# Decoder layer: two heads per output strip and the bias on GpSimd in self-attention; maxima transposed inside the by-key block and fills spread out in cross-attention

## The chip, the cores and the metric

The kernel runs on one core of a Trainium2 chip. The time is device microseconds of one execution. The engines are TensorE (PE; its weight loads are shown as PEld), VectorE (DVE), ScalarE (ACT), GpSimd (POOL) and SyncE (SP), which issues the DMAs. Each has its own instruction stream, and they wait for one another on semaphores.

## The reference

64 sequences of 128 tokens with 128 features, and for each a context of 77 tokens, pass through one decoder layer in float32:

```
x = x + self_attention(layernorm(x))                 # causal, 16 heads of 8, rotary q and k
x = x + cross_attention(layernorm(x), ctx, ctx)
x = x + experts(layernorm(x))                        # top 2 of 8 low-rank experts

self:  out = softmax(q @ k.T * 8**-0.5 + causal) @ v @ Wo + bo
cross: scores = q @ k.T / sqrt(8);  probs = softmax(scores)
       feats = [mean(scores), mean(max_k scores), mean(var_k probs)]   # per sequence and head
       t = exp(clip(mlp(feats), log 0.1, log 10))
       out = softmax(q @ k.T / (2 t)) @ v @ Wo + bo
```

## The kernel before

There are three parts with a barrier between them, and the residual stream X stays on chip: self-attention (about 34 to 547 us), cross-attention (551 to 1285 us) and the experts. The change touches the first two. In both, each engine runs a loop of steps over the 64 sequences, written out by hand: step n does one stage for sequence n, another for n+1, a third for n-3 and so on, and the order of the calls in `step` is the order of the instructions on that engine. A semaphore wait stands at the start of each call. An engine takes its instructions strictly in order.

**Self-attention, step n on PE** (`both_scores`, `pv`, `on_transpose`, `project`, ...). Scores are computed twice, in chunks of 8 heads (h = 0, 1): by query (SQ, to find each row's maximum, with the causal mask added by a matmul, line 436) and by key (SK, from which ACT takes the exponential into P, line 283). Each uses the two PSUM banks of its own tile, so the next chunk's matmuls wait until DVE's maximum (line 356) or ACT's exponential has read the last. P times V goes to O: 16 matmuls of 32 output rows per sequence, where head 4g + j has the strip of rows 32j and the column block g, so O has four blocks of 128 columns. ACT copies O (128x512) to `o`, PE transposes the four blocks (line 485) into R, DVE divides by the sums, PE transposes the result, and `project` adds two products into L: a row of ones times the bias (line 496, contraction over one row) and the output weights (line 497). DVE then adds L to X (line 373) and takes the statistics for the next layer norm. Within a step the order after the first half's P times V is: transpose of xn(n+3), transpose of on(n-2), project(n-3), qkv(n+3), transpose of the maxima(n+1). qkv's stationary operand is xnT, which ACT copies out of PSUM (line 268) after the exponential of chunk 0. POOL makes masked copies of keys and queries, three multiplications a step.

**Cross-attention.** Its parts are split by a lag. For sequence n (`scores_outer`, `scores_inner`) the scores by query go to SQ; DVE takes the row maxima (lines 936, 938) into FEAT; PE transposes them (line 1096) into O; ACT copies them negated into mT (line 809); PE subtracts them from the scores (line 1101); ACT takes the exponential, POOL squares it, DVE sums both. For each group of 8 sequences a small MLP (`mlp1`, `mlp2`, `mlp3`) gives the temperatures. Eleven steps later (LAG) the same sequence is done by key: `by_key(b, h)` is two products of `shift` with `pick` (contraction over 128 rows, line 1112) and three pairs of products over 32 rows (line 1116); then the exponential (line 836), P times V, transpose, norm, projection (lines 1154, 1155). So in steps 0 to 10 only the first half of the work is there, in steps 11 to 63 both, and after that only the second. The maxima of n are transposed before `by_key(n - LAG, 1)`.

ACT's order in a cross step is: exponential of chunk 0, scaled query and row, copies of xcT and o, the maxima (mT), the copies of q, k and v (`qkv_copy`), exponential of chunk 1, copy of onT (line 846), the exponential of the scores.

Before its first step, cross-attention fills its tiles: POOL sets VA (128x7950) and P (128x4096); DVE sets HK, LK, mT and shift, and prepares the MLP's weights; ACT makes `pick`, `heads` and a rounded bias. PE, POOL and DVE each wait for the fills of the others before the first step; DVE's first layer norm (line 920) stands behind all of its own.

Of the kernel before, what the change touches and what calls it, by code (L numbers as in the profile page):

```python
# [15 lines left out]
QUADS, JH = 4, 4  # L16
# [6 lines left out]
def need(eng, sem, value):  # L23
# [10 lines left out]
    headmask=([128, JH], F32, "headmask"), wo=([C, C], F32, "L0_attn_Wo"), bo=([1, C], F32, "L0_attn_bo"),  # L34
# [18 lines left out]
def load_constants(sp, tiles, loaded, constants, dram):  # L53
    for name, (shape, _, source) in constants.items():
# [5 lines left out]
        if name == "b3":  # L60
            src = src.to_broadcast(shape)
# [68 lines left out]
def self_attention(nc, X, ST, MEAN, RSTD, constants, loaded):  # L130

    RING = 4
    ctx = ExitStack()
    with ctx:
# [6 lines left out]
        def sem(name):  # L141
# [4 lines left out]
        ident, identb, identm, future, causal, headmask, cos, sin, wqkv, wo, bo = (  # L146
            constants[n] for n in ("ident", "identb", "identm", "future", "causal", "headmask", "cos", "sin", "wqkv",
                                   "wo", "bo"))
        ones_row = sb("ones_row", [1, T])
# [8 lines left out]
        VA = sb("VA", [128, RING, H, 32])  # L158
# [8 lines left out]
        o = sb("o", [128, QUADS * T])  # L167
# [6 lines left out]
        xn_ready = sem("xn_ready")  # L174
        xnT_ps = sem("xnT_ps")
# [42 lines left out]
        SETS = 3  # L218
        SPLIT = 6
# [17 lines left out]
        def _(pool):  # L237
            nc.gpsimd.memset(VA[:], 0.0).then_inc(const_set, 1)
            pool.wait_ge(const_set, 1)
            nc.gpsimd.memset(VA[:, :, :, DK:DK + 1], 1.0).then_inc(const_set, 1)  # L240
            nc.gpsimd.memset(ones_row[:], 1.0).then_inc(const_set, 1)
# [14 lines left out]

            def step(n, k, i):
                if real(n + 2):
                    masks(n + 2, (k + 2) % RING)

# [3 lines left out]
        def _(act):  # L264
# [5 lines left out]
            def v_copy(b, k):  # L270
                act.wait_ge(rope_part, 3 * (b + 1))
                need(act, pv_ps, 2 * b - 6)
                nc.scalar.copy(VA[:, k, :, 0:DK], M[:, 2 * C:3 * C].rearrange("k (h d) -> k h d", d=DK)).then_inc(v_sb, 1)

# [53 lines left out]
        def _(dve):  # L328
# [30 lines left out]
            def norm(b):  # L359

                dve.wait_ge(oT_ps, b + 1)
                sums = R[:].rearrange("q (h e) -> q h e", e=32)
                nc.vector.reciprocal(rinv[:], sums[:, :, DK]).then_inc(o_rinv, 1)
                dve.wait_ge(o_rinv, b + 1)
                need(dve, onT_ps, b)
                nc.vector.tensor_tensor(on[:].rearrange("q (h d) -> q h d", d=DK), sums[:, :, 0:DK],
                                        rinv[:].unsqueeze(2).to_broadcast([128, H, DK]),
                                        ALU.mult).then_inc(o_norm, 1)
# [33 lines left out]
        def _(pe):  # L402
# [65 lines left out]
            def pv(b, h, k):  # L468
# [4 lines left out]
                for a in range(2):  # L473
                    g = 2 * h + a
                    for j in range(JH):
                        last = mm(O[32 * j:32 * j + 32, g * T:(g + 1) * T], VA[:, k, JH * g + j, :],
                                  P[:, 2 * (k % 2) + h, (JH * a + j) * T:(JH * a + j + 1) * T],
                                  start=(g == 0), stop=(g == QUADS - 1), skip_group_check=True)
# [13 lines left out]
            def project(b):  # L492
# [3 lines left out]
                mm(L[:, T:T + C], ones_row[:], bo[:], start=True, stop=False)  # L496
                mm(L[:, T:T + C], onT[:], wo[:], start=False, stop=True).then_inc(proj_ps, 1)
# [29 lines left out]
def cross_attention(nc, X, ST, MEAN, RSTD, constants, loaded, dram):  # L527

    GROUP = 8
    SLOTS = 2 * GROUP  # L530
    ROUNDS = B // GROUP
    LAG = 11
# [4 lines left out]
    R8 = float(DK) ** 0.5  # L537
    ctx = ExitStack()
    with ctx:
# [66 lines left out]
        const_set = sem("const_set")  # L606
        act_set = sem("act_set")
        pads = sem("pads")
# [54 lines left out]
        SETS = 5  # L663
        PADS = 4
# [15 lines left out]
        def of_group(tile, r):  # L680
            p = r % 2
# [8 lines left out]
        def _(sp):  # L690
# [6 lines left out]
            def rows(b):  # L697
                sp.wait_ge(row_sb, b + 1)
# [7 lines left out]
            sp.wait_ge(pads, PADS)  # L706
# [1164 lines left out]
```

## Time and profile before

| | us |
|---|---|
| median of 3 runs | 1848.47 (1848.45 to 1857.84) |
| profiled execution, its own time | 1853.18 |
| its span | 1851.4 |
| PE busy in the span | 1695.9 |
| DVE busy | 1238.7 |
| ACT busy | 921.6 |
| POOL busy | 848.8 |

The profile is one execution. Busy time is an engine's own; PE's weight loads overlap its matmuls. A matmul's shown time is from its start to the end of its results, so that matmuls that follow one another closely overlap. The clock is TensorE's granted one as a share of 2.4 GHz: 1.00 is 2.4 and 0.50 is 1.2 GHz. Over the whole span its mean is 0.913. In brackets behind a row stands how long the engine was idle just before it and what ended that; `issue` is a time in which the profile shows nothing that it waited for.

### The profile page before, as it was taken

How to read it: one execution, taken by the hardware profiler on the slowest of the kernel's cores; microseconds unless marked ns; L12 is line 12 of the kernel's file. 1: busy time of each engine (PE TensorE's matmuls, PEld its weight loads, DVE VectorE, ACT ScalarE, POOL GpSimd, SP SyncE). 2: the span in 40 equal slices, each digit the busy share in tenths (PEclk: the TensorE clock that was granted, in tenths of full speed). 3: DMA queues.
4: the chain of work that ended last, by engine and by line, in shares of the span. 5: the costliest groups of instructions: out<-in, count | busy, mean ns of one | idle time of the engine just before them, and what ended most of it. 6: DMA issues, size and time to landing. Idle time of an engine off the chain costs nothing. (4 is left out here: it accounts for less than half of the span.)

```text
span 1851.4 us, 42638 instructions
## 1 busy us (share of the span) xinstructions
PE 1695.9 (92%) x14420; PEld 1267.3 (68%) x14420; DVE 1238.7 (67%) x2792; ACT 921.6 (50%) x2143; POOL 848.8 (46%) x892
## 2 busy tenths in 40 slices
PE   0999999999976799999999999886899999999998
PEld 0455555555544566666666666543899999999998
DVE  4666666666655656777777777312777787778776
ACT  1455555555542345666666665433554545454543
POOL 0433444443325556777667776320343344334432
PEclk9999999999985558999999999655899999999999
DMA  5000000000000000000000000000000000000000
GB/s 161 2 2 1 1 1 1 1 1 1 1 6 6 5 4 6 7 7 7 7 6 8 6 7 4 2 2 1 4 7 9 9 9 6 9 9 9 6 9 13
DMA packets 26311, 16.50 MB, mean 9 GB/s; under 512 B 6179, under 2 KB 23525, under 8 KB 26213
## 3 DMA queue, kind: packets, MB, share of 16 engines
q1 hardware_dynamic: 26212, 15.23, 2.9%
q8 instruction: 58, 0.95, 0.2%
q14 instruction: 41, 0.33, 0.1%
HBM read 9.97 MB, written 4.19 MB: 8 GB/s over the span
## 5 line engine op out<-in xcount | busy, mean ns | idle before, releaser
L836 ACT ACTIVATE xa_P<-xa_SK 77x1024 f32<-77x1024 f32 x128 | 130.6, 1020 | 161.8 <-PE xa_SK L1116 161.8
L283 ACT ACTIVATE sa_P<-sa_SK 128x1024 f32<-128x1024 f32 x128 | 131.2, 1025 | 147.2 <-PE sa_SK L426 147.2
L249 POOL TENSOR_TENSOR sa_KM<-sa_HQK,sc_headmask 128x512 fp32r<-128x512 f32 x64 | 66.5, 1039 | 292.1 <-ACT sa_HQK L278 292.1
L1394 POOL TENSOR_TENSOR ff_zz<-ff_zt 128x256 f32<-128x256 f32 x32 | 38.4, 1199 | 319.8 <-DVE ff_zt L1591 319.8
L1462 ACT ACTIVATE ff_SG<-bank 128x512 f32<-128x512 f32 x128 | 76.8, 600 | 192.0 <-PE bank L1664 191.8
L1581 DVE TENSOR_TENSOR ff_GL<-ff_GU,ff_GH 128x512 fp32r<-128x512 f32 x128 | 147.4, 1171 | 27.5 <-ACT ff_GH L1467 27.2
L356 DVE TENSOR_REDUCE sa_mx<-sa_SQ 128x8 f32<-128x1024 f32 x128 | 156.5, 1223 | 6.8 <-PE sa_SQ L426 5.4
L770 POOL TENSOR_TENSOR xa_QMH<-xa_QBH,xc_headmask 128x512 fp32r<-128x512 f32 x64 | 72.7, 1136 | 190.8 <-ACT xa_QBH L826 190.8
L1729 PE MATMUL bank<-fh_r,ff_GH 128*128 128x256 f32 x512 | 148.4, 290 | 0.0
L1662 PE MATMUL bank<-ff_ZH,fh_b 128*128 128x256 f32 x512 | 147.7, 289 | 0.0
L1663 PE MATMUL bank<-ff_ZL,fh_b 128*128 128x256 f32 x512 | 145.1, 283 | 0.0
L1664 PE MATMUL bank<-ff_ZH,fl_b 128*128 128x256 f32 x512 | 144.9, 283 | 0.0
L1731 PE MATMUL bank<-fh_r,ff_GL 128*128 128x256 f32 x512 | 143.6, 280 | 0.0
L728 POOL TENSOR_TENSOR xa_E<-xa_E 128x1232 f32<-128x1232 f32 x64 | 143.1, 2236 | 0.2 <-ACT xa_E L818 0.2
L1730 PE MATMUL bank<-fl_r,ff_GH 128*128 128x256 f32 x512 | 143.0, 279 | 0.0
L1576 DVE TENSOR_TENSOR ff_GU<-ff_SG,bank 128x512 f32<-128x512 f32 x128 | 88.0, 688 | 68.6 <-ACT ff_SG L1462 63.1
L1467 ACT CAST ff_GH<-ff_GU 128x512 fp32r<-128x512 f32 x128 | 79.0, 624 | 55.3 <-DVE ff_GU L1576 32.1
L936 DVE TENSOR_REDUCE xa_FEAT<-xa_SQ 128x12 f32<-128x924 f32 x64 | 71.7, 1121 | 51.8 <-PE xa_SQ L1071 51.6
L1112 PE MATMUL xa_SK<-xa_shift,xa_pick 128*128 128x512 f32 x256 | 104.8, 495 | 0.0
L1402 POOL TENSOR_TENSOR ff_ZH<-ff_AH,ff_M 128x512 fp32r<-128x512 f32 x64 | 83.3, 1302 | 45.9 <-ACT ff_M L1440 45.9
L445 PE MATMUL sa_SK<-sa_shift,sa_pick_row 128*128 128x512 f32 x256 | 103.8, 486 | 0.0
L1663 PEld LDWEIGHTS bank<-ff_ZL,fh_b 128*128 128x128 f32 x512 | 98.4, 192 | 0.0
(257 smaller groups left out, 5444.1 us busy)
## 6 DMA issues: line engine op xcount, KB each, us to landing
xa_shift<-xa_row SPq DMA_DIRECT2D x256, 2.0 KB
out<-X SPq DMA_DIRECT2D x64, 64.0 KB, 1.5
xa_cx<-ctx SPq DMA_DIRECT2D x64, 38.5 KB
sa_shift<-sa_mT SPq DMA_DIRECT2D x64, 8.0 KB, 1.8
fr_b<-L_ffn_B SPq DMA_DIRECT2D x2, 256.0 KB, 3.9
fr_r<-down_a SPq DMA_DIRECT2D x1, 512.0 KB, 4.7
fr_w<-L_ffn_w_gate SPq DMA_DIRECT2D x1, 256.0 KB, 3.5
fr_w<-L_ffn_w_up SPq DMA_DIRECT2D x1, 256.0 KB, 3.6
```

The lines of the kernel that those rows point to most:

```text
L283: nc.scalar.activation(P[:, 2 * (k % 2) + h, :], SK[:], ACT.Exp).then_inc(p_ready, 1)
L356: nc.vector.tensor_reduce(mx[:, p, 2 * JH * h:2 * JH * h + 2 * JH], SQ[:].rearrange("q (j k) -> q j k", k=T), AX.X, ALU.max).then_inc(max_ ...
L728: nc.gpsimd.tensor_tensor(E2[:], E1[:, b % 2], E1[:, b % 2], ALU.mult).then_inc(e2_ready, 1)
L836: nc.scalar.activation(P[0:TC, (2 * b + h) % 4, :], SK[0:TC, :], ACT.Exp).then_inc(p_ready, 1)
L1112: mm(bank(SK, a), pick[:, r // 32], shift[:, b % 2].rearrange("c j t -> c (j t)"), start=True, stop=False)
L1581: nc.vector.tensor_tensor(GG[1][:, k % 4, :], GU[:, k % 2, :], GG[0][:, k % 4, :].bitcast(F32), ALU.subtract).then_inc(gl_done, 1)
L1662: mm(out, w[0], x[0], start=start, stop=False, **kw)
L1663: mm(out, w[0], x[1], start=False, stop=False, **kw)
L1664: return mm(out, w[1], x[0], start=False, stop=stop, **kw)
L1729: mm(out, h, RD[0][:, f, :], start=(s == 0 and f == 0), stop=False, skip_group_check=True)
L1730: mm(out, h, RD[1][:, f, :], start=False, stop=False, skip_group_check=True)
L1731: last = mm(out, l, RD[0][:, f, :], start=False, stop=(s == 1 and f == 3), skip_group_check=True)
```

## The change

In self-attention two heads share a strip of O. V is laid out in two halves per sequence, one for the even heads and one for the odd, with zeros where the other head's columns are, so that the products of both heads add up in the same 32 rows. O then has two blocks of 128 columns, and `o_copy`, `o_transpose` and `norm` follow. The bias is added to X by POOL (`add_bias`), one sequence a step, after xn has been taken; the bias matmul goes, and the residual on DVE waits for POOL as well.

In cross-attention `by_key(b, 1)` takes a function that it calls after its first pair of 32-row products; it holds the transpose of the maxima and the MLP's third product. The fills are spread: POOL sets the V tile of the first four sequences and mT before its first step, the rest of V at step 0, and a quarter of P in each of the steps 1 to 4; DVE prepares the MLP's weights at step 0, splits the bias at step 2 and sets the padding columns of HK and LK and the tile shift at steps 2 to 4; ACT makes `heads` at step -2 and `pick` at step 1. Each has a semaphore of its own, and waits for it where it is first used. Some constants get names (RINGS, HIDDEN) with their values unchanged; the group stays at 8.

```
# self-attention
-        VA = sb("VA", [128, RING, H, 32])
+        VA = sb("VA", [128, RING, 2, PART])            # PART = 265
-        o = sb("o", [128, QUADS * T])
+        o = sb("o", [128, 2 * T])
+            def add_bias(b):                            # POOL
+                pool.wait_ge(xn_ready, b + 1)
+                xb = X[:, bass.ts(b, C)]
+                nc.gpsimd.tensor_tensor(xb, xb, bo_rows[:], ALU.add).then_inc(biased, 1)
             def step(n, k, i):
                 if real(n + 2):
                     masks(n + 2, (k + 2) % RING)
+                if real(n + 1):
+                    add_bias(n + 1)
-                nc.scalar.copy(o[:], O[:]).then_inc(o_sb, 1)
+                nc.scalar.copy(o[:], O[:, 0:2 * T]).then_inc(o_sb, 1)
             def residual(b):
                 dve.wait_ge(proj_ps, b + 1)
+                dve.wait_ge(biased, b + 1)
-                for a in range(2):
-                    g = 2 * h + a
-                    for j in range(JH):
-                        last = mm(O[32 * j:32 * j + 32, g * T:(g + 1) * T], VA[:, k, JH * g + j, :],
...
+                for e in range(2):
+                    for t in range(4):
+                        head = 2 * t + e
+                        at = 256 * e + 32 * (4 * h + t)
+                        last = mm(O[32 * t:32 * t + 32, h * T:h * T + T], VA[:, k].rearrange("k e x -> k (e x)")[:, at:at + 32],
...
-                for g in range(QUADS):
-                    last = tr(R[:, g * T:(g + 1) * T], o[:, g * T:(g + 1) * T], ident[:])
+                for h in range(2):
+                    last = tr(R[:, h * T:(h + 1) * T], o[:, h * T:(h + 1) * T], ident[:])
-                mm(L[:, T:T + C], ones_row[:], bo[:], start=True, stop=False)
-                mm(L[:, T:T + C], onT[:], wo[:], start=False, stop=True).then_inc(proj_ps, 1)
+                mm(L[:, T:T + C], onT[:], wo[:], start=True, stop=True).then_inc(proj_ps, 1)
# cross-attention, by key and the step on PE
+                    if part == 0 and between is not None:
+                        between()
...
-                if real(n):
-                    max_transpose(n)
-                if r is not None:
-                    mlp3(r)
+                def maxima():
+                    if real(n):
+                        max_transpose(n)
+                    if r is not None:
+                        mlp3(r)
                 if real(n - LAG):
-                    by_key(n - LAG, 1)
+                    by_key(n - LAG, 1, maxima)
+                else:
+                    maxima()
# cross-attention, fills
+            values(0, FIRST, 0)                         # POOL, before its steps; FIRST = 4
+            nc.gpsimd.memset(mT[:].bitcast(F32), 0.0).then_inc(mT_set, 1)
...
+                if n == 0:
+                    values(FIRST, VRING, 2)
+                if 1 <= n <= 4:
+                    nc.gpsimd.memset(P[:, n - 1], 0.0).then_inc(p_set, 1)
+                if n == 0:                              # DVE, at the end of its step
+                    prepare()
+                if n == 2:
+                    split_bias()
+                    nc.vector.memset(HK[:, :, TC:T].bitcast(F32), 0.0).then_inc(pads_set, 1)
+                if n == 3:
+                    nc.vector.memset(LK[:, :, TC:T].bitcast(F32), 0.0).then_inc(pads_set, 1)
+                if n == 4:
+                    nc.vector.memset(shift[:].bitcast(F32), 0.0).then_inc(shift_set, 1)
```

PE's order in self-attention, from the second half's P times V to qkv, before and now (line numbers of each kernel's own text; the two middle parts are the other half's scores):

```order
L476 MATMUL sa_O<-sa_P,sa_VA 32x128 x7
L485 MATMUL sa_R<-sc_ident,sa_o 128x128 [waits sa_onT_sb,sa_o_sb]
L485 MATMUL sa_R<-sc_ident,sa_o 128x128 x3
L421 MATMUL sa_M<-sc_ident,sa_qk 128x128 [waits sa_v_sb,sa_qk_roped]
...
L490 MATMUL sa_R<-sc_ident,sa_on 128x128 [waits sa_o_norm]
L496 MATMUL sa_L<-sc_bo,sa_ones_row 128x128 [waits sa_mT_sb,sa_x_done,sa_onT_sb]
L497 MATMUL sa_L<-sc_wo,sa_onT 128x128
L416 MATMUL sa_M<-sc_wqkv,sa_xnT 128x384 [waits sa_xnT_sb]
```

```order
L489 MATMUL sa_O<-sa_P,sa_VA 32x128 x7
L498 MATMUL sa_R<-sc_ident,sa_o 128x128 [waits sa_onT_sb,sa_o_sb]
L498 MATMUL sa_R<-sc_ident,sa_o 128x128
L433 MATMUL sa_M<-sc_ident,sa_qk 128x128 [waits sa_v_sb,sa_qk_roped]
...
L503 MATMUL sa_R<-sc_ident,sa_on 128x128 [waits sa_o_norm]
L509 MATMUL sa_L<-sc_wo,sa_onT 128x128 [waits sa_mT_sb,sa_x_done,sa_onT_sb]
L428 MATMUL sa_M<-sc_wqkv,sa_xnT 128x384 [waits sa_xnT_sb]
```

Two of the four transposes of o and the bias product are gone; their waits stand on what follows.

PE's order in a cross step, from the transposes of o to the subtraction of the maxima, before and now:

```order
L1144 MATMUL xa_R<-xc_ident,xa_o 128x128
L1096 MATMUL xa_O<-xc_ident,xa_FEAT 16x128 [waits xa_o_sb,xa_max_ready]
L1112 MATMUL xa_SK<-xa_shift,xa_pick 128x512 [waits xa_p_ready]
L1112 MATMUL xa_SK<-xa_shift,xa_pick 128x512
L1116 MATMUL xa_SK<-xa_QMH,xa_HK 128x512 x2
L1116 MATMUL xa_SK<-xa_QML,xa_HK 128x512 x2
L1116 MATMUL xa_SK<-xa_QMH,xa_LK 128x512 x2
L1101 MATMUL xa_SQ<-xa_heads,xa_mT 128x462 [waits xa_mT_sb]
```

```order
L1188 MATMUL xa_R<-xc_ident,xa_o 128x128
L1153 MATMUL xa_SK<-xa_shift,xa_pick 128x512 [waits xa_p_ready]
L1153 MATMUL xa_SK<-xa_shift,xa_pick 128x512
L1157 MATMUL xa_SK<-xa_QMH,xa_HK 128x512 x2
L1131 MATMUL xa_O<-xc_ident,xa_FEAT 16x128 [waits xa_o_sb,xa_max_ready]
L1157 MATMUL xa_SK<-xa_QML,xa_HK 128x512 x2
L1157 MATMUL xa_SK<-xa_QMH,xa_LK 128x512 x2
L1138 MATMUL xa_SQ<-xa_heads,xa_mT 128x462 [waits xa_mT_sb]
```

The wait for `xa_max_ready` now stands behind four products instead of ahead of them, and between the maxima's transpose and the subtraction there are four products instead of eight.

POOL's order at the start of cross-attention now:

```order
L735 MEMSET xa_VA 128x2120
L738 MEMSET xa_VA 77x8x8 [waits xa_va_set]
L743 MEMSET xa_mT 128x2048
L775 TENSOR_TENSOR xa_LK<-xa_QK,xa_HK 128x77 [waits xa_h_ready,xc_loaded]
...
L784 TENSOR_TENSOR xa_KML<-xa_LK,xc_headmask 128x308 [waits xa_l_ready]
L735 MEMSET xa_VA 128x5830
L738 MEMSET xa_VA 77x22x8 [waits xa_va_set]
L750 TENSOR_TENSOR xa_E<-xa_E 128x1232 [waits xa_e1_ready]
```

Before, one memset of 7950 columns and one of P stood ahead of the first `xa_LK`; now the larger part of V is set between the masks of step 0 and the first square.

## Rows read from the trace of the kernel before

**Rows 1.** By stretch: us, busy us of PE, PEld, DVE, ACT, POOL, clock, DMA, GB/s
```profile
300.00:400.00 100.00, 100.00 (x948) 59.09 (x943) 69.24 (x158) 50.72 (x105) 40.71 (x41) 1.00 0.01 1
...
660.00:700.00 40.00, 39.43 (x207) 27.45 (x206) 20.52 (x35) 15.64 (x43) 23.32 (x27) 0.50 0.02 6
...
704.00:708.00 4.00, 4.00 (x52) 2.76 (x42) 1.63 (x2) 1.86 (x3) 0.00 (x0) 0.77 0.01 4
...
800.00:900.00 100.00, 93.45 (x873) 63.67 (x873) 73.70 (x146) 65.11 (x171) 72.11 (x88) 0.98 0.03 7
...
1200.00:1240.00 40.00, 36.26 (x217) 20.09 (x217) 5.57 (x20) 12.08 (x24) 8.55 (x8) 0.50 0.01 2
```

**Rows 2.** Timeline, one self step, PE: start us, us, engine, line, op, [idle]
```profile
297.90 0.66 PE L485 MATMUL sa_R<-sc_ident,sa_o 128*128 128x128 f32 x4
...
301.06 0.33 PE L412 MATMUL sa_M<-sc_ident,sa_xn 128*128 128x128 f32 x1
...
301.43 0.48 PE L496 MATMUL sa_L<-sc_bo,sa_ones_row 1*128 1x128 f32 x2
...
301.84 0.49 PE L497 MATMUL sa_L<-sc_wo,sa_onT 128*128 128x128 f32 x2
...
302.06 0.30 PEld L416 LDWEIGHTS sa_M<-sc_wqkv,sa_xnT 128*128 128x128 f32 x2
...
305.52 0.66 PE L485 MATMUL sa_R<-sc_ident,sa_o 128*128 128x128 f32 x4
```

**Rows 3.** Timeline, the same self step: what PE waits for next
```profile
296.99 1.22 DVE L356 TENSOR_REDUCE sa_mx<-sa_SQ 128x8 f32<-128x1024 f32 x1
...
298.50 0.21 PEld L436 LDWEIGHTS sa_SQ<-sc_causal,sc_identb 128*128 128x128 bf16 x2
...
301.60 0.26 ACT L268 COPY sa_xnT<-sa_M 128x128 f32<-128x128 f32 x1
```

**Rows 4.** Timeline, starts of both attention parts, POOL and DVE
```profile
34.15 1.80 POOL L238 MEMSET sa_VA<- 128x2048 f32 x1 [33.70 <-POOLq L74]
...
34.20 1.84 DVE L332 TENSOR_SCALAR sa_xn<-X,MEAN,RSTD 128x128 f32<-128x128 f32 x1 [9.29 <-PEq L74]
...
551.42 6.71 POOL L717 MEMSET xa_VA<- 128x7950 f32 x1
...
563.28 0.33 DVE L920 TENSOR_SCALAR xa_xn<-X,MEAN,RSTD 128x128 f32<-128x128 f32 x1
```

**Rows 5.** Timeline, one cross step, PE
```profile
849.98 0.52 PEld L1101 LDWEIGHTS xa_SQ<-xa_heads,xa_mT 128*128 128x128 f32 x3 [0.36 <-issue]
...
856.33 0.38 PE L1144 MATMUL xa_R<-xc_ident,xa_o 128*128 128x128 f32 x2
...
857.27 0.28 PE L1096 MATMUL xa_O<-xc_ident,xa_FEAT 128*16 128x128 f32 x1 [0.56 <-DVE xa_FEAT L938]
...
857.30 0.71 PE L1112 MATMUL xa_SK<-xa_shift,xa_pick 128*128 128x512 f32 x2
...
857.94 0.50 PE L1116 MATMUL xa_SK<-xa_QMH,xa_HK 32*128 32x512 f32 x2
...
858.84 0.52 PEld L1101 LDWEIGHTS xa_SQ<-xa_heads,xa_mT 128*128 128x128 f32 x3 [0.37 <-issue]
...
860.28 0.32 PE L1154 MATMUL xa_M<-xa_bias,xa_minus_ones 2*128 2x128 f32 x1
```

**Rows 6.** Timeline, the same cross step, ACT
```profile
857.59 0.27 ACT L809 ACTIVATE xa_mT<-xa_O 16x128 fp32r<-16x128 f32 x1 [1.95 <-PE xa_O L1096]
...
858.95 1.02 ACT L836 ACTIVATE xa_P<-xa_SK 77x1024 f32<-77x1024 f32 x1 [0.30 <-PE xa_SK L1116]
...
859.87 0.25 ACT L846 COPY xa_onT<-xa_R 128x128 f32<-128x128 f32 x1
```

**Rows 7.** Timeline, ACT: maxima copies of two neighbouring cross steps
```profile
685.26 0.27 ACT L809 ACTIVATE xa_mT<-xa_O 16x128 fp32r<-16x128 f32 x1 [3.02 <-PE xa_O L1096]
...
699.74 0.27 ACT L809 ACTIVATE xa_mT<-xa_O 16x128 fp32r<-16x128 f32 x1 [3.02 <-PE xa_O L1096]
```

More of the change, by code:

```diff
@@ L730, in similarity @@
             def similarity(r):
-                part = slice(r % 2 * GROUP, r % 2 * GROUP + GROUP)
+                part = slice(r % RINGS * GROUP, r % RINGS * GROUP + GROUP)
                 pool.wait_ge(k_sb, GROUP * (r + 1))
-                need(pool, mlp_ps, 3 * (r - 2) + 1)
+                need(pool, mlp_ps, 3 * (r - RINGS) + 1)
                 nc.gpsimd.tensor_tensor(qk[:], qsum[:, part], ksum[:, part], ALU.mult).then_inc(qk_ready, 1)
@@ L742, in variance @@
                 cols = slice(slot(2 * i) * H, slot(2 * i) * H + 2 * H)
-                need(pool, mlp_ps, 3 * (2 * i // GROUP - 2) + 1)
+                need(pool, mlp_ps, 3 * (2 * i // GROUP - RINGS) + 1)
                 pool.wait_ge(zr_ready, i + 1)
@@ L750, in low @@
             def low(b):
-                need(pool, pads, PADS)
                 pool.wait_ge(h_ready, 2 * b + 2)
@@ L801, in qkv_copy @@
                                      accum_out=ksum[:, s:s + 1]).then_inc(k_sb, 1)
+                if b < VRING:
+                    act.wait_ge(va_set, 2 if b < FIRST else 4)
                 need(act, pv_ps, 2 * (b - VRING) + 2)
@@ L833, in exps @@
                 need(act, pv_ps, 2 * b + h - 3)
-                if b == 0 and h == 0:
-                    act.wait_ge(const_set, SETS)
+                if b < 2:
+                    act.wait_ge(p_set, 4)
                 nc.scalar.activation(P[0:TC, (2 * b + h) % 4, :], SK[0:TC, :], ACT.Exp).then_inc(p_ready, 1)
@@ L849, in gelu1 @@
                 act.wait_ge(mlp_ps, 3 * r + 1)
-                nc.scalar.activation(h1[:], R[0:64, 3 * T:4 * T], ACT.Gelu, bias=b1s[:]).then_inc(mlp_act, 1)
+                nc.scalar.activation(h1[:], R[0:64, HIDDEN], ACT.Gelu, bias=b1s[:]).then_inc(mlp_act, 1)
             def gelu2(r):
                 act.wait_ge(mlp_ps, 3 * r + 2)
-                nc.scalar.activation(h2[:], R[0:64, 3 * T:4 * T], ACT.Gelu, bias=b2[:]).then_inc(mlp_act, 1)
+                nc.scalar.activation(h2[:], R[0:64, HIDDEN], ACT.Gelu, bias=b2[:]).then_inc(mlp_act, 1)
             def inverse_t(r):
@@ L897, in _ @@
                     exp_e(n)
+                if n == -2:
+                    nc.scalar.copy(heads[:].rearrange("h (g k) -> h g k", k=TC),
+                                   ident[:, 0:H].unsqueeze(2).to_broadcast([128, H, TC])).then_inc(heads_set, 1)
+                if n == 1:
+                    nc.scalar.copy(pick[:], rows4.to_broadcast([128, QUADS, T])).then_inc(pick_set, 1)
+                    act.wait_ge(bias_ps, 1)
+                    nc.scalar.copy(bias_high[:], R[0:2, 0:C]).then_inc(bias_sb, 1)
         @block.vector
@@ L932, in row_max @@
                 dve.wait_ge(sq_ps, b + 1)
-                need(dve, mlp_ps, 3 * (b // GROUP - 2) + 1)
+                need(dve, mlp_ps, 3 * (b // GROUP - RINGS) + 1)
                 m = FEAT[:, 1, columns(b)]
@@ L963, in factors @@
             def factors(r):
-                part = slice(r % 2 * GROUP, r % 2 * GROUP + GROUP)
+                part = slice(r % RINGS * GROUP, r % RINGS * GROUP + GROUP)
                 dve.wait_ge(mlp_act, 3 * r + 3)
-                need(dve, row_sb, GROUP * (r - 1))
+                need(dve, row_sb, GROUP * (r - RINGS + 1))
                 nc.vector.tensor_scalar(CF[:], CF[:], math.exp(-LOG_T_MAX), None, ALU.max).then_inc(clipped, 1)
@@ L1103, in subtract_max, with by_key @@
                 last.then_inc(neg_ps, 1)
-            def by_key(b, h):
+            def by_key(b, h, between=None):
                 need(pe, p_ready, 2 * b + h)
+                if b == 0 and h == 0:
+                    pe.wait_ge(pads_set, 2)
+                    pe.wait_ge(shift_set, 1)
+                    pe.wait_ge(pick_set, 1)
                 if h == 0:
@@ L1161, in mlp1 @@
                 need(pe, onT_sb, n - LAG - 1)
+                if r == 0:
+                    pe.wait_ge(prepared, PREPARED + 1)
                 for f in range(3):
-                    last = mm(R[0:64, 3 * T:4 * T], w1s[:, f, :], of_group(FEAT[:, f], r), start=(f == 0), stop=(f == 2))
+                    last = mm(R[0:64, HIDDEN], w1s[:, f, :], of_group(FEAT[:, f], r), start=(f == 0), stop=(f == 2))
                 last.then_inc(mlp_ps, 1)
```

134 lines of the change are left out of this document (69 added, 65 removed).

## The prediction

> **What bounds the kernel now.** I read first the table by stretch, because the share over the whole span mixes stages that have different limits. In self-attention PE is busy all of the time and the other engines are not near it: DVE 69 us of 100, ACT 51, POOL 41 [rows 1]. So whatever PE issues there is paid for, until the next wait comes up. In the main part of cross-attention PE is busy 93 us of 100, and the rest is one wait, which repeats in each step. Between the two lies a stretch at 0.50 of the clock (1.2 GHz): the fills, the first steps of cross-attention, and about three of its full steps; the clock is back inside the stretch that starts at 704 us. The end of cross-attention (1200 to 1240 us) is at 0.50 again.
>
> Next I read the timeline of one step of each part, to see what stands behind PE. A self step takes 305.52 - 297.90 = 7.62 us [rows 2]. A cross step at 2.4 GHz takes 858.84 - 849.98 = 8.86 us, and PE idles 0.56 us in it, ahead of the transpose of the row maxima [rows 5].
>
> All sums are made against the profiled execution: 1853.18 us, with a span of 1851.4. The median of the runs is 1848.47, 4.7 us below it; I carry the difference over to the median unchanged.
>
> **Self: transposes of o, four to two.** Four take 0.66 us and one alone takes 0.33 [rows 2], so each one more costs (0.66 - 0.33) / 3 = 0.11, and two fewer save 0.22 us a step. Is PE held by something else 0.22 us earlier? The next instruction with a wait is the causal matmul: its weights load at 298.50, and the row maxima that free its bank end at 296.99 + 1.22 = 298.21 [rows 3]. A hand-over takes about 0.04 (the maxima transpose ends at 857.27 + 0.28 = 857.55 and ACT starts at 857.59 [rows 5, 6]). So the load moves to 298.28, and 298.25 would be its limit: the whole 0.22 is kept, but no slack is left. The product P times V keeps its count and its shape (two heads add into one strip, where each had its own), so it costs nothing. ACT's copy of o is halved, but that comes behind the copies for which PE waits.
>
> **Self: the bias matmul leaves PE.** From its first pass at 301.43 to the projection at 301.84 are 0.41 us [rows 2]. Behind it stand the projection and then the weights load of qkv, at 302.06, and this needs xnT, which ACT has ready at 301.60 + 0.26 = 301.86 [rows 3]. With 0.04 for the hand-over, qkv can't load before 301.90: only 302.06 - 301.90 = 0.16 of the 0.41 is gained, the rest becomes a wait for ACT, which is not free because it does an exponential ahead of that copy. (ACT's chain hangs on PE's score product, so it moves along with the 0.22 above.) The bounds are 0 and 0.41. I take 0.16, since the copy's end is a row and nothing in the change moves it. The addition goes to POOL, which is 59% idle there; the trace has no such operation in self, but even one as long as its 1.80 us memset [rows 4] fits, and the sequence's sum is wanted three steps later. The added wait in the residual stands ahead of the statistics on DVE and is met long before.
>
> Self together: (0.22 + 0.16) x 62 steps (of 64, the first and the last not being full ones) = 23.6 us. Bounds: 0.22 x 62 = 13.6, if the bias gives nothing, and 0.63 x 62 = 39.1.
>
> **Cross: the fills.** Now the first normalised x is ready at 563.28 + 0.33 = 563.61 [rows 4]; DVE's memsets and the weight preparation come before it. In the changed kernel it is DVE's first instruction. It won't start at once: in self-attention the same operation, started beside POOL's memset of 1.80 us, took 1.84 us instead of 0.33 and ended 0.09 after it [rows 4]. The Trainium skill (GPSIMD Engine Reference, Specifications) says that GpSimd's SBUF interfaces are shared with VectorE, with contention in its 2-port modes; the trace agrees by that 1.84. POOL's first VA memset now has 2120 columns, at 6.71 us / 7950 = 0.844 ns each, so it ends at 551.42 + 1.79 = 553.21, and x is ready at 553.3. Gain: 10.3 us. The price: POOL's second VA memset (5830 columns, 4.9 us) lies in step 0, behind the masks, and pushes the square, DVE's casts and its sum behind it by 1 us or so. Even with the full steps of 660 to 700 us DVE is idle 19.5 of 40 us and POOL 16.7 [rows 1], so most of it is made good in the next step. The P memsets are 1024 x 0.844 ns = 0.9 us each in POOL's idle time. I take off 0.5 and keep 9.8. Bounds: 7 (the memset's delay reaches PE in two steps) and 10.3.
>
> **Cross: maxima inside the second by-key block.** Now PE stops until 857.27 for the maxima. In the changed order the two mask products with shift, which need 857.94 - 857.30 = 0.64 to the next load [rows 5], start right behind the transposes of o, at 856.33 + 2 x 0.11 = 856.55, and the first product pair loads at 857.19 minus the little that the overlapping of the transpose took: 857.1. It lasts 0.50 [rows 5]. Then comes the price. At each change of the tile's rows PE's load waits for the pair in front to end: the load at 857.94 starts 0.07 before 857.30 + 0.71 = 858.01. The change adds two such points, before and behind the maxima transpose. So: transpose at 857.1 + 0.50 - 0.07 = 857.53, end 857.81 (the maxima are there at 857.23, no wait); next pair loads at 857.74, ends 0.50 later at 858.24; the last pair 0.23 later at 858.47; subtraction loads at 858.40, where it was 858.84. PE alone would gain 0.44.
>
> The Trainium skill (TensorEngine Tiling, Key Properties) says that changing the tiling mode, not just the tile, drains TensorE. The trace agrees by the 0.37 us idle ahead of the load at 858.84 [rows 5]. By the rule alone the two new drains of 0.37 would take back 0.74, more than the 0.56 that goes.
>
> But ACT is next. Its copy of the maxima moves from 857.59 to 857.85, by 0.26; behind it come the q, k and v copies and the exponential at 858.95, before which ACT idles 0.30 [rows 6]. So the exponential starts at 858.95 - 0.30 + 0.26 = 858.91, and the copy of onT, which ended at 859.87 + 0.25 = 860.12, ends at 860.08. The bias product that needs it starts at 860.12 in place of 860.28 [rows 5]: 0.16 a step. The bounds are -0.1 (the new drains cost 0.1 more than I read and ACT passes all on) and 0.44. I take 0.16, times 48 steps at 2.4 GHz: 7.7 us (bounds -5 and 21). In the three full steps at 1.2 GHz there is no wait to remove (39.43 of 40 us busy [rows 1]) and the two drains are pure loss, about 0.5 each: 1.5 us. The tail has no maxima: nothing.
>
> **Sum:** 23.6 + 9.8 + 7.7 - 1.5 = 39.6 us. Profiled about 1813.6, median 1848.5 - 39.6 = 1808.9 us.
>
> **The rivals.** (B) PE gets all that it is freed of: ACT's copies aren't last because its earlier work moves up too. 39.1 + 9.8 + 21 - 1.5 = 68 us, 1780. For it: ACT is only half busy; against it: the two hand-overs of [rows 3, 6]. (C) The time turns into waits: only the transposes count in self (13.6), the drains eat the gain in cross (-5), the fills give 7, less 1.5: 14 us, 1834. For it: there is no slack at 298.25, and the causal matmul may now wait; the shared port makes POOL's new addition and fills hold DVE. (D) slower: the clock comes back later. A cross step takes 699.74 - 685.26 = 14.48 us at 1.2 GHz [rows 7] against 8.86: 5.6 us for each step that the clock is late. PE was busy 39.43 of the 40 us before 700 and still at half clock [rows 1], so the return hangs on little, and the by-key block, dense before, now has two drains in it. From 7 steps late on the 40 us are gone; with 10 late it is 1848.5 - 40 + 56 = 1865 us. Against it: what PE executes in a step hardly differs. (E) the clock comes back up to three steps earlier: 17 us more, 1792. (F) The change doesn't do what it says, and another wait takes the place of that for the maxima without any gain: this is inside C.
>
> **How the numbers follow.** Forecast 0.60 (its own range 1797 to 1821), B 0.12, C 0.15, D 0.05, E 0.08. The range 1784 to 1832 leaves out about half of B, half of C, and D: under 0.2. A measurement of this kernel can tell about 0.5%, or 9 us, from no change. Faster by more than that: the forecast, B, E and most of C, 0.91; within it, a bad C or a D of five to eight steps, 0.04; slower, 0.05.
>
> **What would show it.** Self: a step of 7.24 us, two transposes of o, no bias product, and a new PE wait of about 0.25 us at qkv for ACT's xnT. Cross start: the first normalised x ready at 10.3 us less behind the start of its part than now, held by POOL's memset. Cross: a step of 8.70 us, no wait for the maxima, idle time of PE's loads on both sides of the maxima transpose, ACT without idle ahead of the second exponential, and PE waiting for the copy of onT. Wrong would be: a self step under 7.1 or over 7.4 us; a cross step under 8.5 or not under 8.86; or a stretch at half clock whose end does not move with the start of cross-attention.

## The result: 1794.05 us, about 58 us faster

The changed kernel took 1794.05 us (median of 4 runs, 1785.59 to 1797.58) beside 1852.47 for the kernel before in the same runs: ratio 0.968, interval 0.963 to 0.973. The forecast was 1808.9, with 1784 to 1832 as its range: right in sign, and the range held the time, but the gain was forecast at 39.6 us, and the time lies under the 1797 to 1821 that the prediction gave its main case. A second set of four runs of the same kernel gave 1802.16 (1793.78 to 1810.57), so the eight times together have a median of 1797 and a spread of 25 us. How much of a gain is the change and how much is such a spread is the main question of the experiments.

The profiled execution of after took 1791.54 us (span 1789.7), 61.6 less than the one of before. By stretch, in the columns of [rows 1]:

```profile
300.00:400.00 100.00, 96.68 (x925) 56.23 (x935) 74.20 (x168) 50.04 (x112) 48.05 (x57) 1.00 0.01 1
660.00:680.00 20.00, 19.80 (x181) 13.16 (x180) 15.09 (x30) 11.27 (x34) 16.71 (x21) 1.00 0.03 7
...
720.00:820.00 100.00, 97.68 (x924) 65.68 (x925) 74.58 (x148) 63.44 (x173) 76.06 (x95) 1.00 0.03 7
...
1130.00:1210.00 80.00, 72.52 (x432) 40.19 (x432) 11.42 (x41) 24.17 (x48) 17.12 (x16) 0.50 0.01 2
```

In self PE is no longer busy all of the time: a wait has appeared. In cross it idles less than before, 2.3 us of 100 in place of 6.5. At 660 us, where [rows 1] had 0.50, the clock is back at 2.4 GHz. The tail of cross is still at 1.2 GHz.

The self step of after (a timeline, all engines), which answers to [rows 2, 3]:

```profile
299.76 0.49 PE L438 MATMUL sa_SQ<-sa_KM,sa_HQK 32*128 32x512 f32 x2
...
301.50 0.39 PE L509 MATMUL sa_L<-sc_wo,sa_onT 128*128 128x128 f32 x2
...
301.76 0.26 ACT L276 COPY sa_xnT<-sa_M 128x128 f32<-128x128 f32 x1
...
302.07 0.30 PEld L428 LDWEIGHTS sa_M<-sc_wqkv,sa_xnT 128*128 128x128 f32 x2 [0.37 <-ACT sa_xnT L276]
302.07 0.91 PE L428 MATMUL sa_M<-sc_wqkv,sa_xnT 128*128 128x384 f32 x2 [0.18 <-ACT sa_xnT L276]
...
302.46 0.46 POOL L261 TENSOR_TENSOR X<-X,sc_bo_rows 128x128 f32 x1
...
305.39 0.44 PE L498 MATMUL sa_R<-sc_ident,sa_o 128*128 128x128 f32 x2
...
306.90 0.50 PE L438 MATMUL sa_SQ<-sa_KM,sa_HQK 32*128 32x512 f32 x2
```

The step is 306.90 - 299.76 = 7.14 us, and over 44 steps the copies of onT are 7.16 apart, where they were 7.60. Two transposes of o take 0.44, POOL's addition 0.46, and PE waits for ACT's xnT ahead of qkv.

The start of cross in after, which answers to [rows 4]:

```profile
527.05 2.18 DVE L946 TENSOR_SCALAR xa_xn<-X,MEAN,RSTD 128x128 f32<-128x128 f32 x1 [0.55 <-PEq L74]
...
527.29 1.86 POOL L735 MEMSET xa_VA<- 128x2120 f32 x1
```

POOL's short memset ends at 529.15 and the first normalised x is ready at 529.23, 1.94 us behind the memset's start; before it was 563.61 - 551.42 = 12.19 [rows 4].

A cross step of after, which answers to [rows 5, 6]:

```profile
788.05 0.38 PE L1188 MATMUL xa_R<-xc_ident,xa_o 128*128 128x128 f32 x2
...
788.83 0.50 PE L1157 MATMUL xa_SK<-xa_QMH,xa_HK 32*128 32x512 f32 x2
...
789.26 0.09 PEld L1131 LDWEIGHTS xa_O<-xc_ident,xa_FEAT 128*16 128x16 f32 x1 [0.24 <-issue]
789.26 0.28 PE L1131 MATMUL xa_O<-xc_ident,xa_FEAT 128*16 128x128 f32 x1
...
789.57 0.27 ACT L838 ACTIVATE xa_mT<-xa_O 16x128 fp32r<-16x128 f32 x1 [2.20 <-PE xa_O L1131]
...
790.12 0.52 PEld L1138 LDWEIGHTS xa_SQ<-xa_heads,xa_mT 128*128 128x128 f32 x3 [0.36 <-ACT xa_mT L838]
...
790.53 1.01 ACT L865 ACTIVATE xa_P<-xa_SK 77x1024 f32<-77x1024 f32 x1
...
791.45 0.24 ACT L875 COPY xa_onT<-xa_R 128x128 f32<-128x128 f32 x1
...
791.74 0.32 PE L1200 MATMUL xa_M<-xa_bias,xa_minus_ones 2*128 2x128 f32 x1
...
796.64 0.38 PE L1188 MATMUL xa_R<-xc_ident,xa_o 128*128 128x128 f32 x2
```

There is no wait for the maxima; their transpose stands in the by-key block, with 0.24 us idle ahead of its load. ACT starts the exponential without idle time, and the product with the bias comes 0.05 us behind the copy of onT. The step is 8.59 us where it was 8.86.

### The profile page after: what moved, and what is told of

It is laid out like the page before. It is cut to its first block and busy times, and to the rows that moved or that the text cites. A ratio compares the mean times of both kernels' runs of the same rounds, so it can differ in the third digit from the quotient of the medians.

```text
span 1789.7 us, 42209 instructions
## 1 busy us (share of the span) xinstructions
PE 1650.3 (92%) x14102; PEld 1229.0 (69%) x14164; DVE 1229.8 (69%) x2791; ACT 898.0 (50%) x2143; POOL 879.9 (49%) x961
## 5 line engine op out<-in xcount | busy, mean ns | idle before, releaser
L457 PE MATMUL sa_SK<-sa_shift,sa_pick_row 128*128 128x512 f32 x256 | 99.8, 471 | 0.2 <-ACT sa_P L293 0.2
```

## The experiments: parts of the change

All are compared with the kernel before in the same runs; steps are the distances between ACT's copies of onT (self, a mean over 44 steps) or of the maxima (cross) in each profile. In cross, steps 0 to 10 are called fill steps, those from 11 on by-key steps, and those from 64 on, which have no maxima any more, the tail. An MLP pair is a step with an MLP and the one after it.

**Self alone.** Changed self-attention, old cross-attention.

> The changed self-attention in front of the old cross-attention. Theory S (the gains of the parts add, and the slow first steps of self belong to its new start): a self step of 7.17 us in place of 7.60, the first steps at half clock as in the changed kernel, so the end of self 23 us earlier and the whole about 23 us faster (ratio 0.988). Rival (the slow first steps were chance): clock up at about 51 us as before, the whole 28 to 29 us faster. In cross the step stays 8.86 us. If the earlier return of the clock in cross comes from the time at which cross starts, it shows here too and gives about 14 us more; if it comes from the fills or the order in cross, the first three by-key steps stay at 13 to 14 us each.

Measured: 1823.73 us against 1852.1, ratio 0.985 (0.981 to 0.988), so 28 us. Self step 7.16, cross step 8.85. The first copy of onT came at 78.8 us.

**Strips alone.** The kernel with self alone, with the bias back on PE (and without POOL's addition and its wait):

```diff
-                mm(L[:, T:T + C], onT[:], wo[:], start=True, stop=True).then_inc(proj_ps, 1)
+                mm(L[:, T:T + C], ones_row[:], bo[:], start=True, stop=False)
+                mm(L[:, T:T + C], onT[:], wo[:], start=False, stop=True).then_inc(proj_ps, 1)
```

> Of the change only the two heads per strip in self (two transposes of o in place of four); the bias stays a product on PE. The prediction's step: 0.22 us a step less, 7.38 us, 13.6 us in all. Rival (the product of P and V also costs something, or ACT is what holds the step): between 0 and 0.15 less. Rival that the 0.44 measured for both edits together belongs mostly to the strips: 0.28 or more less, a step of 7.32 us or under.

Measured: 1841.82 us, ratio 0.994 (0.992 to 0.997). Step 7.43: the strips give 7.60 - 7.43 = 0.17 us, and the bias, by difference from 7.16, gives 0.27.

**Fills alone.** Old self-attention and the changed cross-attention, with `maxima()` called ahead of `by_key(n - LAG, 1)`.

> Old self-attention, the changed start of cross-attention (fills spread over the first steps), the transpose of the maxima ahead of the second by-key block as before. Start of cross 10.9 us earlier, steady step 8.86 us. If the fills bring the clock back earlier: by-key steps at full clock from the first, another 14 us, ratio 0.986. If it is the new place of the maxima that does it: three by-key steps of 13 to 14 us stay, and only 11 us come out, ratio 0.994.

Measured: 1842.49 us, ratio 0.997 (0.994 to 0.999), so 6 us by the ratio, with 1 to 11 us in its interval. From the last copy of onT to the first copy of the maxima 21.33 us instead of 31.68: 10.35 earlier. The first cross step is 0.1 us longer, and the next nine have the same lengths as before to 0.01 us.

**Maxima alone.** The old kernel with this edit, and with the call in `by_key` that the changed kernel has:

```diff
-                if real(n):
-                    max_transpose(n)
-                if r is not None:
-                    mlp3(r)
+                def maxima():
+                    if real(n):
+                        max_transpose(n)
+                    if r is not None:
+                        mlp3(r)
...
                 if real(n - LAG):
-                    by_key(n - LAG, 1)
+                    by_key(n - LAG, 1, maxima)
+                else:
+                    maxima()
```

> The old kernel with one edit: transpose of the maxima (and the third MLP product) inside the second by-key block. Steady cross step 8.59 us instead of 8.86; with the MLP steps half a us longer, some 8 us in all. If this order also brings the clock back earlier, another 14 us and about 4 at the last two steps: 26 us, ratio 0.986. If not, the three half-clock steps stay, each 0.5 us longer: 7 us, ratio 0.996.

Measured: 1839.34 us, ratio 0.992 (0.989 to 0.996). Step 8.59. The MLP steps got longer: 10.31 where they were 9.80. Three slow steps stayed: 10.35, 13.82 and 10.78 us.

The medians of the parts add to 28 + 10 + 13 = 51 us (49 by the ratios). The two sets of the whole gave 58 and 52 us by their medians (60 and 56 by the ratios).

**The changed kernel again.**

> The changed kernel once more, unaltered, to separate what its first profile owes to chance. Steps at 2.4 GHz must repeat to 0.02 us: self 7.15, cross 8.59, MLP pair 10.3 and 10.2. Theory K (the moment at which the clock comes back varies from run to run): it comes somewhere between 85 and 120 us after the first copy of the maxima, by-key steps 1 to 3 may cost 5 us each more than in the first profile, and the self start may be 5 us earlier. Rival: the clock comes back 90 to 91 us after it again, fixed by the new order of the fills.

Measured: 1802.16 us (1793.78 to 1810.57). Its profile took 1810.57, 19 us more than the first profile of the same program. ACT's copies of the maxima in the steps in question:

```profile
634.44 0.27 ACT L838 ACTIVATE xa_mT<-xa_O 16x128 fp32r<-16x128 f32 x1 [4.36 <-PE xa_O L1131]
648.26 0.27 ACT L838 ACTIVATE xa_mT<-xa_O 16x128 fp32r<-16x128 f32 x1 [4.69 <-PE xa_O L1131]
663.12 0.27 ACT L838 ACTIVATE xa_mT<-xa_O 16x128 fp32r<-16x128 f32 x1 [4.69 <-PE xa_O L1131]
677.98 0.27 ACT L838 ACTIVATE xa_mT<-xa_O 16x128 fp32r<-16x128 f32 x1 [4.69 <-PE xa_O L1131]
692.83 0.27 ACT L838 ACTIVATE xa_mT<-xa_O 16x128 fp32r<-16x128 f32 x1 [4.68 <-PE xa_O L1131]
```

and two stretches of PE there (columns of [rows 1]):

```profile
650.00:690.00 40.00, 40.00 (x231) 26.91 (x230) 16.93 (x32) 15.50 (x39) 18.90 (x25) 0.50 0.01 4
690.00:694.00 4.00, 4.00 (x17) 2.28 (x16) 1.46 (x7) 1.17 (x7) 1.03 (x1) 0.67 0.03 10
```

Steps of 14.86 us at 1.2 GHz where the first profile had 8.59: PE was busy without a gap and the clock came back only within the second stretch, at 692.6. The moment of the return, counted from the first copy of the maxima: 130 us (before), 111 (self alone), 110 (strips), 102 (fills), 116 (maxima), 91 and 155 (the changed kernel twice), and 111 and 91 in two kernels below that are the changed one up to there. So 102 to 130 with the old order of the maxima and 91 to 155 with the new: the values overlap, and 155 lies outside the 85 to 120 that were expected. From the 12th copy of the maxima to the 17th it took 57.1 us in the profile of before, 42.3 and 67.0 in the two of the changed kernel. So the 14.8 us that the first profile saved there can't be put down to the change. The same holds for the start of self: the first copy of onT came at 74 us in the profile of before, at 80 in the first of after, at 76 in the second, and at 80 and 79 where self was the old code.

**The end of cross.** One more stretch of these profiles differs, and here the two orders don't overlap. The 62nd copy of the maxima and the last copy of onT, before and after:

```profile
1144.96 0.27 ACT L809 ACTIVATE xa_mT<-xa_O 16x128 fp32r<-16x128 f32 x1 [1.94 <-PE xa_O L1096]
1283.68 0.27 ACT L846 COPY xa_onT<-xa_R 128x128 f32<-128x128 f32 x1 [1.93 <-PE xa_R L1149]
```

```profile
1088.45 0.27 ACT L838 ACTIVATE xa_mT<-xa_O 16x128 fp32r<-16x128 f32 x1 [2.19 <-PE xa_O L1131]
1221.66 0.27 ACT L875 COPY xa_onT<-xa_R 128x128 f32<-128x128 f32 x1 [1.93 <-PE xa_R L1193]
```

That is 138.7 us before and 133.2 after. The other three profiles with the old order have 145.8 (self), 139.4 (strips) and 138.7 (fills), the other two with the new one 133.1 (maxima) and 130.4 (the changed kernel again). The last eight steps take 74.8 us in all of them, and the two steps ahead of the last scores explain about 1 us. The rest goes with the time at 1.2 GHz: 117 to 137 us of that stretch with the old order, 99 to 108 with the new. Why the clock falls there later or less often isn't shown.

## The experiments: what the new order costs in the MLP steps

In the changed kernel the MLP step (ACT and PE):

```profile
760.87 0.36 ACT L883 ACTIVATE xa_h<-xa_R,xc_b 64x128 f32<-64x128 f32 x1 [0.32 <-PE xa_R L1216]
762.17 0.27 ACT L838 ACTIVATE xa_mT<-xa_O 16x128 fp32r<-16x128 f32 x1 [0.94 <-PE xa_O L1131]
...
763.25 1.28 ACT L865 ACT_TABLE_LOAD   x1
764.55 1.02 ACT L865 ACTIVATE xa_P<-xa_SK 77x1024 f32<-77x1024 f32 x1
...
765.67 0.25 ACT L875 COPY xa_onT<-xa_R 128x128 f32<-128x128 f32 x1
...
765.97 0.32 PE L1200 MATMUL xa_M<-xa_bias,xa_minus_ones 2*128 2x128 f32 x1 [0.76 <-ACT xa_onT L875]
```

and in the kernel before:

```profile
811.65 0.36 ACT L854 ACTIVATE xa_h<-xa_R,xc_b 64x128 f32<-64x128 f32 x1 [0.32 <-PE xa_R L1168]
811.91 0.25 ACT L809 ACTIVATE xa_mT<-xa_O 16x128 fp32r<-16x128 f32 x1
...
814.27 1.02 ACT L836 ACTIVATE xa_P<-xa_SK 77x1024 f32<-77x1024 f32 x1
```

From the second activation to the copy of the maxima it was 0.26 us and is now 1.30. Behind that copy stand q, k, v, a table load of 1.28 us, the exponential and the copy of onT, and at its end PE now waits 0.76 us.

> The changed kernel, except that in the seven steps with an MLP the transpose of the maxima and the third MLP product stand ahead of the by-key block, as in the old kernel. Theory A (in those steps ACT's copy of the maxima moved 1 us back, and behind it come the q, k and v copies, the table load, the exponential and the copy of onT for which PE waits 0.76 us): first MLP step 9.8 us instead of 10.3, the pair 20.0 or less, 3.5 us in all, plain steps stay 8.59. Rival (it is the two added drains that cost, and the wait replaces another): the pair stays at 20.5.

Measured: first MLP step 9.28 us, better than the old 9.80. But 1795.76 us, no faster than the changed kernel beyond the spread: the second step of the pair was 10.5 to 13.1 us, and the clock fell in five of the six rounds beside by-key steps (in each profile of the changed kernel in three). In the round where it held, the pair was 9.27 and 10.50. PE's two waits in an MLP step, and then two stretches, this step and the fall behind it:

```profile
767.31 0.49 PE L1216 MATMUL xa_R<-xa_h,xa_w2p 64*128 64x128 f32 x2 [0.45 <-ACT xa_h L879]
...
768.25 0.48 PE L1220 MATMUL xa_R<-xa_h,xa_w3r 64*128 64x128 f32 x2 [0.24 <-ACT xa_h L883]
```

```profile
760.00:768.00 8.00, 7.46 (x78) 5.12 (x76) 5.94 (x11) 6.07 (x12) 6.33 (x10) 1.00 0.02 4
768.00:772.00 4.00, 3.75 (x16) 2.35 (x16) 1.31 (x6) 3.65 (x10) 2.94 (x5) 0.72 0.04 10
```

## The experiments: keeping PE busy

These ask whether PE's waits decide when the clock falls and returns. The edit in all of them is a loop of products whose output nobody reads; the copies of the maxima and `heads` are their operands. In the versions from "all together" on they go into SK, all but the 12 in a row behind a wait until ACT has read that bank.

```diff
+            def keep_busy(tile, columns, count):
+                for _ in range(count):
+                    mm(tile, mT[:, 0], heads[:, 0:columns], start=True, stop=True)
```

**In the fills.** `keep_busy(SK[:, 0:462], 462, 3)` behind `subtract_max(n)` in steps 0 to 10.

> The changed kernel; PE gets three idle products more (462 columns, into the still unused bank of SK, their output read by nobody) in each of the 11 cross steps ahead of the first by-key block, in the place where it now waits 1.44 us for ACT. Theory D (the clock comes back once PE is busy without these gaps): back to 2.4 GHz some steps earlier than 85 us after the first maxima copy, by-key steps 1 to 3 at 8.6 us; 0 to 15 us faster than the changed kernel, depending on when that one gets its clock back. Rival (the gaps don't decide, or these products don't fit): no earlier, fill steps longer than 8.33 us, up to 15 us slower.

Measured: 1801.38 us (1794.55 to 1812.97). Fill steps as long as before (8.33), so the products cost nothing, but the clock came back 90 us after the first copy of the maxima, fell again after 3, and was back at 110, with no further fall until the first MLP pair. No gain that the spread lets one see.

**In the tail.** `keep_busy(SQ[:, 0:462], 462, 5)` ahead of the transposes of o where `n >= B`, behind a wait until ACT has read the last scores.

> The changed kernel; PE gets five idle products more (462 columns, into the bank of SQ, which nobody reads any more) in each step after the last scores, where it waits 0.94 us a step for ACT's copy of o at half clock. Theory D (these gaps hold the clock down for the 110 us of the tail): clock at 2.4 GHz in most of the tail, a tail step of 6 to 7 us instead of 10.05, 20 to 40 us faster. Rival (something else holds the clock): it stays at 1.2 GHz and each of the 11 steps gets about 1 us longer, 10 us slower.

Measured: 1767.60 us (1766.18 to 1772.71), 30 below the 1797 of the changed kernel's eight runs and 35 below the four taken beside it. In its tail (columns of [rows 1]):

```profile
1120.00:1180.00 60.00, 54.64 (x485) 32.48 (x483) 14.25 (x49) 27.80 (x53) 17.72 (x19) 1.00 0.01 2
```

A tail step of the changed kernel, and the five products in this one:

```profile
1152.82 0.69 PE L1188 MATMUL xa_R<-xc_ident,xa_o 128*128 128x128 f32 x2 [0.94 <-ACT xa_o L870]
...
1162.86 0.69 PE L1188 MATMUL xa_R<-xc_ident,xa_o 128*128 128x128 f32 x2 [0.94 <-ACT xa_o L870]
```

```profile
1147.64 0.44 PE L1188 MATMUL xa_R<-xc_ident,xa_o 128*128 128x128 f32 x2
...
1153.32 1.33 PE L1229 MATMUL xa_SQ<-xa_heads,xa_mT 128*128 128x462 f32 x5
1154.76 0.44 PE L1188 MATMUL xa_R<-xc_ident,xa_o 128*128 128x128 f32 x2
```

Just ahead of that stretch there was one fall, from 1096 to 1112 us. A tail step took 7.12 us where it was 10.04. PE's share is the same as in the row above for 1130 to 1210, 0.91; the clock is 1.00 instead of 0.50.

**All together**: the MLP steps of the last section, 3 and 1 idle products in them, 5 in each tail step, 3 in the two steps ahead, 12 in a row at step 10.

> The changed kernel with four additions: in the steps with an MLP the maxima ahead of the by-key block; idle products on PE (462 columns into the bank of SK, nobody reads them) in those steps where PE waits (3 ahead of the second MLP product, 1 ahead of the third); 5 in each tail step and 3 in the two steps ahead of the tail; and 12 in a row at the end of step 10, just ahead of the first by-key block. Theory D (gaps in PE's work decide when the clock falls and returns): clock back within 10 us of that burst, by-key steps 1 to 3 at 8.6, MLP pair 9.3 and 10.2 in every round without a fall of the clock, tail at 2.4 GHz from its start: 1755 us or less. Rival (only the tail's gain is real): 1768 as the tail alone gave, or more.

Measured: 1762.22 us (1760.21 to 1764.29), ratio 0.951 (0.947 to 0.955), where 1755 or less was expected. MLP pairs 9.39 and 10.49 in all six rounds, the clock at 2.4 GHz without a break from 648 us until the end of the tail at 1197. The 12 products:

```profile
624.56 4.07 PE L1231 MATMUL xa_SK<-xa_heads,xa_mT 128*128 128x462 f32 x12
```

They did not do what they were to do: the clock, which had been up from 614 to 617 already, was up at 628, fell at 634 and came back at 648, and a by-key step of 13.74 us stayed.

**Without the 12 products.**

> The same without the 12 idle products in a row at step 10. Theory D: the clock comes back between 90 and 155 us after the first maxima copy, as chance has it, and up to three by-key steps cost 5 to 6 us more each; otherwise step for step like the kernel with the burst. The burst itself costs 4.6 us at 1.2 GHz less what PE would have waited, so on average 0 to 8 us slower without it. Rival: without it no slower, or faster by the 3 to 5 us of the burst.

Measured: 1769.88 us (1759.95 to 1779.77), the clock back 104 us after the first copy. Two of the four runs are as fast as the full version, two are 14 to 18 us slower at a lower clock.

**MLP steps as in the changed kernel.**

> Burst and tail as in the full version, but the MLP steps as in the changed kernel (maxima and third product inside the by-key block, no idle products there). Theory: MLP pair 10.3 and 10.2 to 11.9 (the clock falls in some of the rounds), against 9.3 and 10.2 where they are moved and filled: 7 to 12 us slower than the full version over the 6 rounds beside by-key steps. Rival: the pairs come out alike, the difference under 3 us.

Measured: 1772.07 us (1771.39 to 1775.37), 10 slower than the full version. The pairs were 10.3 to 10.5 and 10.2 to 11.8 us, and the clock fell in four of the six rounds.

**The tail's products in the bank of SQ.** In the full version they wait 0.54 us a step for ACT's exponential to leave SK.

```diff
+            def keep_busy_tail(count):
+                pe.wait_ge(e1_ready, B)
+                for _ in range(count):
+                    mm(SQ[:, 0:462], mT[:, 0], heads[:, 0:462], start=True, stop=True)
```

> The full version again, with one difference: in the tail steps the 5 idle products go into the bank of SQ, which is free, instead of SK, where they wait 0.54 us for ACT's exponential. Theory: a tail step of 7.12 us (as the kernel with the tail alone had) instead of 7.39, 3 us faster than the full version, 1759 us, with the clock as high and the four times within 5 us of each other. Rival: without the wait the products end too early and PE waits for the copy of o again, so that the clock falls in the tail: 1780 us.

Measured: 1758.67 us (1758.51 to 1760.87), ratio 0.950 (0.948 to 0.951): the fastest kernel here, 95 us below the one before and about 38 below the changed kernel. A tail step takes 7.11 us. Its profile had one fall of the clock, from 1116 to 1126 us.

## Why the prediction was right, and where its sizes were off

**Self, transposes: right.** 0.22 forecast, 0.17 measured. PE gets its 0.22 back at the transposes: in the strips kernel the next product starts 0.28 behind their start, in before 0.49. Up to the score products behind the causal one (299.60 in the step of [rows 2]) it is 1.55 instead of 1.70, so some of it is lost where the forecast itself saw no slack.

**Self, bias: the mechanism right, the term mis-sized.** The forecast was 0.16 a step and a new wait of 0.25 for xnT. The wait is there, 0.18 on PE and 0.37 on its loads, but the gain is 0.26 to 0.27. The step that failed was to read the gain at the load of the weights (302.06 before): that load did come earlier by about what was forecast, from 2.46 us behind the score products to 2.31. Before, that load lay beside the projection still running, and its product started only at 302.17; without the bias product both start together. From the score products of the step (299.60) to the qkv product it was 302.17 - 299.60 = 2.57, and it is now 302.07 - 299.76 = 2.31. ACT's copy ends 2.26 behind them in both: ACT was the bound, as said. The two rows of before that tell it, PE in the step of [rows 2]:

```profile
299.60 0.50 PE L426 MATMUL sa_SQ<-sa_KM,sa_HQK 32*128 32x512 f32 x2
...
302.17 0.81 PE L416 MATMUL sa_M<-sc_wqkv,sa_xnT 128*128 128x384 f32 x2
```

Together 0.44 a step times 64 is 28 us, as the kernel with self alone measured, against 23.6.

**Fills: right.** Forecast 10.3 earlier by POOL's memset, with the normalisation 0.09 behind its end; measured 10.25 and 0.08. Of the 0.5 taken off for later delays nothing is seen beyond 0.1 us in the first step. The runs with the fills alone are not sharp enough to tell 10 us from 6.

**Maxima: place right, size off both ways.** The transpose starts 1.21 us behind the transposes of o (forecast 857.53 - 856.33 = 1.20), and ACT's copy 1.52 behind (forecast 1.52). The exponential then starts 0.96 behind that copy, not 1.06: with the copies back to back they take 0.10 less than the old rows less their idle time gave. So 0.27 a step, not 0.16. The two added changes of tile cost what the old rows showed (0.24 us idle ahead of the transpose's load), not the 0.37 each that would have made the step longer than before. The Trainium skill (TensorEngine Tiling, Key Properties) says that changing the tiling mode drains TensorE; the idle rows agree that each change costs, but the step came out shorter, not longer. The MLP steps were counted as gaining 0.16 each; the first of each pair loses 0.5 instead (9.80 to 10.31), and the second gains nothing. That had not been priced at all, since no row of an MLP step was read. In eight steps: 6 x 0.27 - 0.5 = 1.1 us, or 7 for the part at full clock, beside 7.7 forecast. A size too small and a cost left out nearly cancelled. A step at half clock grew from 14.48 to 14.86, 0.4 where 0.5 was taken.

**The tail: the term put at nothing.** The prediction says that the tail has no maxima and gains nothing. Its steady steps are indeed the same, but the end of cross as a whole was 5.5 and 8.4 us shorter in the two profiles of the changed kernel than in before, and 5.7 with the maxima alone, with less of it at 1.2 GHz. How the new order would do that stays open.

**The half clock.** One of the prediction's own signs of being wrong came: a stretch at half clock whose end does not move with the start of cross-attention. The first copy of the maxima came 34 and 39 us earlier than before, the return of the clock 73 and 13 us earlier.

**The rivals.** The first set of runs, 1794, is nearest to E's 1792, and the first profile shows E's mechanism (the clock back up to three steps earlier), 14 us of its 61.6. But the second profile of the same kernel has the return 155 us after the first copy, later than any other, so E was met by luck: no run shows that it is an effect of the change. D, a slower kernel, did not come, though its mechanism is what the second profile has. B's full amount did not come, since both waits for ACT named in the forecast are there.

**The sum.** By steps the change is worth 28 + 10 + 7 + about 1 at the last two full-clock steps - 1 in the slow ones = 45 us, and with the end of cross about 50. The medians say 52 and 58. That the forecast of 39.6 lies under both has causes that were sized too small (self, 4.4 us) or put at nothing (the end of cross, about 5); the few us above 50 can't be told from the spread of the return.

## What to carry to other kernels

Read a gain on PE at the product, not at the load of its weights: here the load lay beside the product before it, and moved by 0.15 us where its product moved by 0.26. Where a step has variants (here one in eight with an MLP), price the edit on a row of each variant. Profile the same kernel twice before putting a difference of clock down to the change. And look at the stretches at 1.2 GHz before shaving steps at 2.4: in this kernel 1.3 us of idle products per tail step gave 30 us, about as much as the whole self part.

## What the hardware showed

The share of time that PE is busy does not tell its clock. At 1.2 GHz it stayed for 40 us with 40.00 of 40 busy; in the tail 0.91 busy went with 0.50 in one kernel and with 1.00 in another, the same steps with idle products in the place of PE's wait for o. In the MLP step the clock fell behind waits of 0.45 and 0.24 us in five of six rounds, and with four idle products in these waits in none of 18 (three profiles); with the 12 products and those of the tail but none in these waits it fell in four of six. What decides the return after the fills isn't shown: with the products in the fills it was at 110 us for good, with the 12 in a row at 91, 112 and 113, and without either between 91 and 155. It varies from run to run, 91 and 155 us after the first copy of the maxima for one program. The Trainium skill (TensorE: Matmul & The Clock Gate, Part 1) says that the warm-up differs from run to run of the same kernel; the two profiles agree with that.

The versions with the 12 products lay within 2.4, 4.0 and 4.1 us (4 runs each), the one without them within 19.8; but the kernel with the tail's products alone, without the 12 as well, lay within 6.5. So it isn't shown that the 12 products narrow the spread.
